# Turning the order of two layer norms' rows at a layer's end, and centring h on VectorE

## The reference, cut to what matters

```
e = c * ((diag * h) @ W) + h                 # first layer (W, c for users and items)
h2 = adj @ (adj.T @ e)
x = x + layernorm(h2) * gamma + beta + h
h = relu(layernorm(x)); x = x + adj @ h       # second layer
h = relu(layernorm(x)); x = x + chebyshev(h)  # third: three products with adj
h = relu(layernorm(x)); x = x + relu(dis * ((adj + I) @ (dis * (h @ W3 + b3))))
```

## Time and profile before

| what | value |
|---|---|
| median of three runs | 1488.74 us (1488.53 to 1488.76) |
| the profiled execution's own time | 1489.6 us |
| its span (first to last instruction) | 1487.7 us |
| PE busy | 1463.4 us (98%) |
| DVE busy | 377.6 us (25%) |
| ACT busy | 257.2 us (17%) |
| POOL busy | 84.2 us (6%) |
| mean granted TensorE clock | 0.999 |

### The profile page before, as it was taken

One profiled execution on the slowest core, in us unless ns is written; L12 is line 12 of the kernel. 1 busy time (PEld: TensorE's weight loads), 2 busy tenths in 40 slices (PEclk: granted clock), 3 DMA queues, 4 the chain that ended last, 5 costly groups with the idle time before them and its releaser, 6 DMA issues.

```text
span 1487.7 us, 17934 instructions
## 1 busy us (share of the span) xinstructions
PE 1463.4 (98%) x7901; PEld 628.6 (42%) x7901; DVE 377.6 (25%) x383; ACT 257.2 (17%) x510; POOL 84.2 (6%) x67
## 2 busy tenths in 40 slices
PE   6999999999999999999999999999999999999998
PEld 4555555555555664333333333333333333333332
DVE  6583443454354334110110200000000011101121
ACT  3334343343433452000000000000000000000000
POOL 2210000000000018100000000000000000000000
PEclk9999999999999999999999999999999999999999
DMA  9999999999999998999996787989797848996997
GB/s 331 380 415 394 383 395 384 392 379 396 389 383 367 354 409 319 421 420 420 420 420 217 302 336 294 360 323 317 287 320 275 303 161 336 345 385 228 353 421 305
DMA packets 101777, 522.18 MB, mean 351 GB/s; under 512 B 19228, under 2 KB 19268, under 8 KB 55108
## 3 DMA queue, kind: packets, MB, share of 16 engines
q1 hardware_dynamic: 94612, 519.36, 90.1%
q10 hardware_dynamic: 7088, 1.67, 0.5%
HBM read 414.83 MB, written 106.17 MB: 350 GB/s over the span
## 4 chain that ended last, share of the span: by engine, by line
PE 95%; DMA 4%; DVE 1%; ACT 0%; issue 0%; ACTq 0%; POOL 0%; POOLq 0%; DVEq 0%
PE turned L527 34%; PE acc L527 33%; PE turned L553 12%; PE t_acc L538 12%; DMA staged<-adj_t 3%; PE t_acc L667 1%; PE turned L693 1%; DMA w_in<-in_L_gnn_W_i_dram 0%; PE t_rows L677 0%; PE turned L699 0%; PE acc L579 0%; PE t_acc L601 0%; PE t_rows L601 0%; PE t_rows L592 0%; ACTq L749 0%
## 5 line engine op out<-in xcount | busy, mean ns | idle before, releaser
L741 ACT ACTIVATE staged<-turned 128x512 f32<-128x512 f32 x360 | 183.7, 615 | 251.9 <-PE turned L553 251.4
L875 DVE TENSOR_REDUCE deg_part<-raw 128x4 f32<-128x3072 f32 (+1 forms) x70 | 220.4, 3192 | 0.0
L553 PEld LDWEIGHTS turned<-ident,raw 128*128 128x128 f32 x1600 | 173.6, 140 | 43.3 <-issue 43.3
L553 PE MATMUL turned<-ident,raw 128*128 128x128 f32 x1600 | 191.2, 275 | 0.0
L538 PE MATMUL t_acc<-raw,E 128*64 128x384 f32 (+1 forms) x1120 | 184.4, 474 | 0.0
L527 PE MATMUL acc<-staged,t_cur 128*64 128x512 f32 x720 | 167.7, 601 | 0.1
L527 PE MATMUL turned<-over_last,C 128*64 128x512 f32 x664 | 150.4, 593 | 0.0
L527 PE MATMUL turned<-over_last,R 128*64 128x512 f32 x616 | 139.9, 594 | 0.4 <-DMA over_last<-adj_t 0.4
L538 PEld LDWEIGHTS t_acc<-raw,E 128*64 128x64 f32 x1120 | 79.9, 138 | 103.9 <-issue 98.5
L1049 POOL TENSOR_TENSOR rstd<-rstd,minus_half 128x8 f32<-128x8 f32 (+1 forms) x30 | 44.2, 1474 | 1295.0 <-DVE rstd L866 1295.0
L527 PE MATMUL acc<-over_last,C 128*64 128x512 f32 x416 | 93.9, 593 | 0.0
(11 more groups left out here) (133 smaller groups left out, 804.6 us busy)
## 6 DMA issues: line engine op xcount, KB each, us to landing
over_last<-adj_t SPq DMA_DIRECT2D x177, 1024.0 KB, 8.2
staged<-adj_t SPq DMA_DIRECT2D x93, 1024.0 KB, 9.6
raw<-in_adj_dram SPq DMA_DIRECT2D x60, 1536.0 KB, 15.6
adj_t<-staged SPq DMA_DIRECT2D x60, 1536.0 KB, 12.6
over_wide<-adj_t SPq DMA_DIRECT2D x24, 1024.0 KB, 8.9
raw<-in_adj_dram SPq DMA_DIRECT2D x10, 1024.0 KB, 11.8
adj_t<-over_last SPq DMA_DIRECT2D x8, 1024.0 KB, 8.5
adj_t<-C SPq DMA_DIRECT2D x2, 1024.0 KB, 15.0
```

Source lines behind the costliest of these rows:

```text
L553: last = nc.tensor.transpose(turned[q % TURN_BANKS][:, a * P:(a + 1) * P], raw_of(g, u // 2 * 2 + b)[:, sub, c * P:(c + 1) * P], ident[:, :])
L741: nc.scalar.activation(turned_into(g, u)[:, i * B:(i + 1) * B], turned[q % TURN_BANKS][:, :], ACT.Copy) \
L875: nc.vector.tensor_reduce(deg_part[:, of(m), g], raw_of(g, m), AX.X, ALU.add).then_inc(deg_summed, 1)
```

## The change

The matrix `centring` goes, with the four GpSimd instructions that make it. `rows_of_h` becomes four plain transposes with `ident`. VectorE centres the rows out of PSUM into E, with the `centre` that it uses for x, and ScalarE squares what lies in E and no longer copies. For the fourth block (m = 3, unit 8) the transposes stand behind unit 8's product. In `LN_H`, and so on GpSimd, x of block m - 1 comes ahead of h of block m. ScalarE and VectorE take them in the same order; VectorE centres h before the variance of x. In the diff the first `end_of_layer` is ScalarE's, the second VectorE's.

```diff
-            LN_H += [("h", m)] * (m < ROWS) + [("x", m - 1)] * (m >= 1)
+            LN_H += [("x", m - 1)] * (m >= 1) + [("h", m)] * (m < ROWS)
...
-                    last = nc.tensor.matmul(aux[m % 2][:, a * P:(a + 1) * P], h_acc[:, m, a * P:(a + 1) * P],
-                                            centring[:, :], start=True, stop=True)
+                    last = nc.tensor.transpose(aux[m % 2][:, a * P:(a + 1) * P], h_acc[:, m, a * P:(a + 1) * P], ident[:, :])
...
-                    if g + 1 == NG and u >= 2 and u % 2 == 0:
+                    if g + 1 == NG and turns and u >= 2 and u % 2 == 0:
                         rows_of_h(u // 2 - 1)
...
                              u % 2 == 0, u % 2 == 1).then_inc(used, 1)
+                    if g + 1 == NG and not turns and u % 2 == 0:
+                        rows_of_h(u // 2 - 1)
...
             def square(row, v, out):
-                if row[0] == "h":
-                    act.wait_ge(h_rows, row[1] + 1)
-                else:
-                    act.wait_ge(centred, CENTRED_NO[row] + 1)
+                act.wait_ge(centred, LN_NO[row] + 1)
...
             def end_of_layer(v):
-                m = (v - 2) // 2
-                if v % 2 == 0 and 0 <= m < ROWS:
-                    act.wait_ge(h_rows, m + 1)
-                    nc.scalar.activation(E[:, of_pair(m), :], aux_rows[m % 2], ACT.Copy)
-                    if m >= 2:
-                        act.wait_ge(var_ready, LN_NO["h", m - 2] + 1)
-                    square(("h", m), aux_rows[m % 2], sq[m % 2][:, :, :])
                 m = (v - 4) // 2
                 if v % 2 == 0 and 0 <= m < ROWS:
                     if m >= 2:
                         act.wait_ge(var_ready, LN_NO["x", m - 2] + 1)
                     square(("x", m), E[:, of_pair(m), :], cen[m % 2][:, :, :])
+                m = (v - 2) // 2
+                if v % 2 == 0 and 0 <= m < ROWS:
+                    if m >= 2:
+                        act.wait_ge(var_ready, LN_NO["h", m - 2] + 1)
+                    square(("h", m), E[:, of_pair(m), :], sq[m % 2][:, :, :])
...
             def end_of_layer(v):
                 m = (v - 2) // 2
                 if v % 2 == 0 and 0 <= m < ROWS:
-                    variance(("h", m), sq[m % 2][:, :, :], of_pair(m))
+                    dve.wait_ge(h_rows, m + 1)
+                    centre(("h", m), aux_rows[m % 2], of_pair(m), E[:, of_pair(m), :])
                 m = (v - 4) // 2
                 if v % 2 == 0 and 0 <= m < ROWS:
                     variance(("x", m), cen[m % 2][:, :, :], of_pair(m))
+                m = (v - 2) // 2
+                if v % 2 == 0 and 0 <= m < ROWS:
+                    variance(("h", m), sq[m % 2][:, :, :], of_pair(m))
```

More of the change, by code:

```diff
@@ L243, in gnn_stack @@
         ident = sb("ident", [P, P])
-        centring = sb("centring", [P, P])
         cen = [sb(f"cen{i}", [P, CH, D]) for i in range(2)]
@@ L347, in gnn_stack @@
         for m in range(ROWS + 1):
-            LN_H += [("h", m)] * (m < ROWS) + [("x", m - 1)] * (m >= 1)
+            LN_H += [("x", m - 1)] * (m >= 1) + [("h", m)] * (m < ROWS)
         LN_PASS = [(p, m) for p, m in plan.rows if p in WEIGHED]
         LN_NO = {x: i for i, x in enumerate(LN_START + LN_H + LN_PASS)}
-        CENTRED_NO = {x: i for i, x in enumerate([x for x in LN_START + LN_H + LN_PASS if x[0] != "h"])}
         Y_READ_NO = {}
@@ L555, in turn_unit @@
                     last.then_inc(chunk_turned, 1)
-            pe.wait_ge(made, 3)
+            pe.wait_ge(made, 2)
             pe.wait_ge(diag_in, 16 * 2)
@@ L1038, in _ @@
             chain.step(op.memset(minus_half[:, :], -0.5))
[L1039 to L1043, removed]
             def raise_variances(rows, t):
```

## The result

The changed kernel runs in 1498.23 us (median of 4 runs, 1496.89 to 1499.91) against 1488.75 us: ratio 1.0061, 95% interval 1.0049 to 1.0073. That is 9.5 us slower, where 9.7 were forecast. The profiled execution is the fastest of the four, 1496.89 us, 7.3 us above the profiled one before (1489.6 us); what follows is read from it.

A forecast was written before the change was run, and what follows sets the result against it. TensorE, holding 95% of the chain, was taken as the bound, with a tile's load setting a stretch near the last group. Tile 3's +10.18 us less 2.31 gave +7.87; +1.8 for the clock made +9.7: median 1498.4 us, range 1494 to 1502.

The forecast's parts named there:

- The loop: Last group, from X ready to the next block's X ready across VectorE and GpSimd: 10.76 us against TensorE's 8.0 us.
- additions: VectorE's additions to h_acc that TensorE waits for before blocks 3 and 4: forecast near 569.5 and 580.3 us.
- The idle time before tile 3: TensorE waiting for ScalarE's square of h's block 4: 4.9 us idle, tile 3 starting at 589.96 us.
- the term that decides: x's power ahead of h's in GpSimd's queue closes a cycle of 10.76 us a block.
- Which stall counts: Of TensorE idle stretches of 1.5, 6.6 and 4.9 us, the sum used tile 3's start, +10.18 us.
- Loads: TensorE's four load waits in the first row of pass 0, 2.31 us, would vanish, leaving +7.87 us.
- The rival that loads give nothing back: Load queue restarts as full as today: +9.9 us, up to +12.4 with the clock, 1498.7 to 1501.1 us; chance 0.12.
- The clock: TensorE's idle stretches bring the 1.2 GHz level before tile 3: +1.8 us, ends 0 and 2.47.
- the first stall: TensorE idle 6.6 us before block 4's rows of h, waiting for VectorE's last addition.
- the rival without the clock: Clock stays at 2.4 GHz since tiles 1 and 2 run between the stalls: +7.9 us, 1496.6 us; chance 0.2.
- Transposes: On TensorE, four transposes replace eight centring records per row block of h: 0.475 against 0.89 us, 0.42 us less.
- The saving: TensorE's gain from dropped centring products and a covered 0.80 us wait: about 3 us by the group's end, taken alone.

The follow-up runs named there:

- e2: Kernel before the change with only the order turned, x ahead of h on GpSimd, ScalarE and VectorE: ratio 1.0045.
- e1: Changed kernel with the old order, h ahead of x of the block before, on GpSimd, ScalarE and VectorE: 1495.0 us, ratio 1.0040.
- e5: Changed kernel with the old order, and VectorE centring h ahead of its wait for X: 1487.94 us, ratio 0.9992.
- e7: Changed kernel with VectorE's last addition to h_acc ahead of its wait for X of block 2: 1499.39 us, ratio 1.0075.
- e10: The changed kernel itself, unaltered, run again beside a kernel with filler transposes: 1500.33 us, ratio 1.0067.
- e9: Changed kernel with 50 and 38 filler transposes of the identity in TensorE's two stalls: 1498.02 us, ratio 1.0061.
- e6: Kernel of e5 with the fifth block's rows in step 2 and TensorE's wait for their square ahead of tile 8: 1487.61 us, ratio 0.9995.

## Why the prediction was right

- **The loop**: 10.76 us a block summed, 10.72 in the chain. X ready, additions (569.50 and 580.26 forecast, 569.61 and 580.33 in the trace) and tile 3 (589.96 forecast, 590.00) came within 0.2 us. The idle time before tile 3 did not, 2.19 us for 4.9: the sum let tiles 1 and 2 run at full pace.
- **What the loop was put down to** was half right. I called the turned order the term that decides. e2 shows that it suffices (10.2 us a block), but e1 shows that VectorE's centring behind its wait for X suffices too (9.95 us). I had counted that centring, 1.33 us, as a term of one loop; undoing only the order would still leave 7.6 of 10 us at tile 3. Only with both undone is the kernel's pace back (e5).
- **Which stall counts**: the sum went by the last wait, and e7 confirms it.
- **Loads**: 2.31 us were taken as given back. The shift of tile 3 (+10.0 us by distance from the rows) becomes +7.6 us at tile 20, so 2.4 us came back, and all four waits are gone. The rival that loads give nothing back falls. The tail gives back 0.5 us more (tile 20 starts 7.8 us later on the clock of the trace, the span grows by 7.3): the last tiles wait 0.62 us for one load instead of 0.35 and 0.64.
- **The clock**: +1.8 us was taken, midway between 1.13 and 2.47. It is 0 in the profile of the change, 1.69 and 2.03 us in those of e10 and e7. That the size came out is luck: no row of before priced the lower level (the slow first products, 1.13 us, ran at a granted clock of 1.00), and 2.47 was an assumption on how long it lasts. The mechanism was half right: the first stall did bring the level down, but tiles 1 and 2 paid for it inside the wait; at tiles 3 and 4 it was low again in e10's profile and not in the change's. The profiled execution took 1496.89 us where 1499.3 was summed for it, and 1.8 of these 2.4 us are the clock's part that it did not have. It has the size of the rival without the clock (1496.6 us forecast for the median), though not its reason: the clock did not stay at 2.4 GHz, it fell and came back. The Trainium skill ("TensorE: Matmul & The Clock Gate", What's actually happening) has it that idling brings the throttle and activity releases it; e9 (1.00 with TensorE kept at work) and e10 (0.50 in the long stall) agree.
- **How close the median came** is in part luck too. Its four runs lie at 1496.89 (the profiled one) and 1497.34 us, and at 1499.12 and 1499.91, so the median, 1498.23, falls into the gap between them. In e10's rounds the same kernel loses 10.2 us (1500.33 against 1490.18), so an agreement to 0.2 us is more than the runs can tell.
- **Transposes**: 0.42 us saved a block were summed, 0.46 shown (0.99 to 0.53 us between neighbours). By the Trainium skill's factor of four ("TensorE: Matmul & The Clock Gate", Terms) the estimate would have been 0.67 (0.89 to 0.22); the measurement decides.
- **The saving meant little**: e5 shows 1.1 us at tile 3, e6 2.8, of the 3 us that I had put on it. Neither is told from the kernel before by its interval.

## What to carry to other kernels

When a hand-over between in-order queues is turned, write the loop down: start at one signal, follow every instruction that stands between it and the same signal of the next block, on whatever engine, and compare the sum with the pace of the bounding engine. Do so for each part of a change by itself, since two parts can each close a loop and undoing one then brings little back. Put an operation whose data come early ahead of a wait that comes late in the same queue, and price the stall by the last wait in the chain, not by the sum of the idle stretches.

## What the runs showed of the hardware

After 6.48 us of idle time in the change's profile TensorE's four transposes take 1.12 us instead of 0.66, and the granted clock is 0.50 while they run. Whether a second, shorter wait brings the lower level back differed between executions of one kernel: a stretch of 2.19 us idle left the clock at 1.00, one of 3.21 us (e10) let it fall to 0.50 about 1 us after work had begun again. The length of the wait alone does not decide it: in e2 3.54 us idle before block 4's rows left 1.00 from 580 to 586 us, and the 3.38 us before tile 3 were followed by 0.50 from 590 to 592. The reduce and the centring operation read from PSUM in the same 0.69 us as from SBUF.
